# Gate passes of a graph GRU on 64-row halves of TensorE, with the x load, the xs load and the h copy moved

## The reference

```
adj = relu(x.reshape(b, 1600) @ masker_param + masker_bias)      # (b, 2, 50, 50)
adj = adj / (adj.sum(-1) + 1e-6)
m = adj @ (h @ weight)                                            # h starts as x
gates = m @ w_ih.T + b_ih + h @ w_hh.T + b_hh
r, z, ng = split(gates, 3)
h = (1 - sigmoid(z)) * tanh(sigmoid(r) * ng) + sigmoid(z) * h
h = batch_norm(h); h = layer_norm(h)
out = softmax(h @ attn_w.T + attn_b) @ h                          # (b, 2 * 32)
```

## Time and profile before

| | us |
|---|---|
| median of 3 runs (2510.01 to 2519.66) | 2515.34 |
| the profiled execution | 2501.48 |
| its span in the profile | 2499.7 |
| TensorE busy in the span | 2353.0 (94%) |
| VectorE, ScalarE, GpSimd busy | 1052.6, 817.7, 560.5 |
| granted TensorE clock, mean | 0.971 |

### The profile page before, as it was taken

The page is one execution under the profiler, slowest core; times in us unless marked ns, Lnnn a source line. Parts: engine busy times, 40 slices in busy tenths (PEclk is TensorE's granted clock), DMA queues, the critical chain, the costliest instruction groups (busy, mean ns, idle before and its releaser), DMA issues. The chain is left out here.

```text
span 2499.7 us, 34838 instructions
## 1 busy us (share of the span) xinstructions
PE 2353.0 (94%) x12466; PEld 1906.7 (76%) x12466; DVE 1052.6 (42%) x1787; ACT 817.7 (33%) x1369; POOL 560.5 (22%) x365
## 2 busy tenths in 40 slices
PE   8999999999999999999999966999999999965788
PEld 7888888888888888888888855888888888852333
DVE  5333222333352223333123313656666566674456
ACT  4222221222242222222122213445454444436340
POOL 0000000000000000000000000677676777764230
PEclk9999999999999999999999987999999999977899
DMA  6322122222242222211222024545555454327430
GB/s 219 118 86 85 31 81 86 86 86 86 80 147 88 86 86 84 84 55 59 86 86 83 28 72 133 159 137 162 154 148 161 134 168 139 117 82 224 125 91 5
DMA packets 137728, 264.14 MB, mean 106 GB/s; under 512 B 11590, under 2 KB 97382, under 8 KB 134374
## 3 DMA queue, kind: packets, MB, share of 16 engines
q1 hardware_dynamic: 121546, 237.24, 30.5%
q10 hardware_dynamic: 16128, 26.22, 3.0%
HBM read 195.72 MB, written 67.70 MB: 105 GB/s over the span
## 5 line engine op out<-in xcount | busy, mean ns | idle before, releaser
L344 PE MATMUL psum<-w_hi,x_lo 128*128 128x500 f32 x2080 | 820.9, 395 | 8.1 <-DVE w_lo L214 8.1
L344 PE MATMUL psum<-w_lo,x_hi 128*128 128x500 f32 (+1 forms) x2080 | 810.3, 390 | 0.0
L344 PE MATMUL psum<-w_hi,x_hi 128*128 128x500 f32 x1920 | 745.9, 388 | 0.0
L278 DVE TENSOR_REDUCE rows<-u 128x10 f32<-128x500 f32 x160 | 107.6, 672 | 917.5 <-ACT u L227 917.2
L344 PEld LDWEIGHTS psum<-w_hi,x_lo 128*128 128x128 f32 x2080 | 391.4, 188 | 83.8 <-issue 8.4
L344 PEld LDWEIGHTS psum<-w_lo,x_hi 128*128 128x128 f32 (+1 forms) x2080 | 392.0, 188 | 75.1
L344 PEld LDWEIGHTS psum<-w_hi,x_hi 128*128 128x128 f32 x1920 | 360.8, 188 | 73.2
L233 ACT COPY at<-psum 128x640 f32<-128x640 f32 x160 | 110.9, 693 | 699.5 <-PE psum L324 699.5
L638 POOL MEMSET share<- 128x1 f32 x1 | 0.1, 98 | 1484.2 <-POOLq L82 1484.2
L704 PE MATMUL psum<-adj_sb,xs_sb 100*64 100x100 f32 x2048 | 200.6, 350 | 32.5 <-DMA xs_sb<-xz 32.5
L227 ACT ACTIVATE u<-psum 128x500 f32<-128x500 f32 x160 | 94.0, 587 | 332.7 <-PE psum L344 332.7
(11 more groups left out here) (170 smaller groups left out, 2878.2 us busy)
## 6 DMA issues: line engine op xcount, KB each, us to landing
w_raw<-W SPq DMA_DIRECT2D x140, 500.0 KB, 6.8
adjT<-at SPq DMA_DIRECT2D x320, 125.0 KB
adj_sb<-adjT SPq DMA_DIRECT2D x16, 2500.0 KB
xs_sb<-xz SPq DMA_DIRECT2D x16, 1600.0 KB
hF<-hC ACTq DMA_DIRECT2D x96, 256.0 KB, 2.8
h<-hF SPq DMA_DIRECT2D x64, 256.0 KB, 4.1
xg_sb<-xg SPq DMA_DIRECT2D x16, 800.0 KB, 18.8
h<-hF SPq DMA_DIRECT2D x48, 192.0 KB, 3.7
```

The source lines that it names most:

```text
L278: nc.vector.tensor_reduce(rows[:, 0], u[:, c2], AX.X, ALU.add).then_inc(dve_step, 1)
L344: last = nc.tensor.matmul(mm_out(w % 2), a[0:r, k, cols], b[0:r, k, :], start=k == 0 and n == 0, stop=k == KF and n == 1)
```

## The change

1. **R and Z in row halves.** The weights of R and Z are packed in one array `wd[:, :, RZ_W]`: rows 0 to 63 (two blocks) hold R in columns 0 to 63 and Z in columns 64 to 127, rows 64 to 127 hold Z in columns 0 to 63 and R in columns 64 to 127. Each of the six products is issued twice, on rows 0 to 63 and on rows 64 to 127, with outputs in two banks, so 12 products of 64 rows take the place of 12 of 128. N stays as it was, now last, with the transposes ahead of it. Semaphores `rz_done` and `gates_done` take the place of one per gate, and the R/Z products wait for both sigmoids of the step before.
2. **ScalarE** does each sigmoid in two instructions of 64 partitions, from the two banks. The result of Z goes to one bank, so it first waits for the h of the step before (`h_ready`).
3. **The h copy** (`evacuate`) moves from ScalarE to VectorE, between `update` and `finish`; `store` moves behind tanh.
4. **The load of `xg`** is issued by ScalarE's queue, behind tanh of round 0 of the next tile, and no more by SyncE.
5. **`xs`** has the layout [100, 2, 2, 32, 64] and is loaded as two transfers of 50 partitions by 8 KB each for a tile, half of the bytes. The zeros are set once at the start by VectorE, and SyncE waits for them. A weight load now reads its 64 columns at a distance of 64 elements.

```diff
-        xs = sb("xs_sb", [2 * N, 2, SH, 2 * D])
+        xs = sb("xs_sb", [2 * N, 2, 2, D, SH])
...
-                sp.dma_start(xs[:, r], ins["xz"][tile]).then_inc(adj_loaded[r], 16)
+                for half in range(2):
+                    sp.dma_start(xs[N * half:N * half + N, r, half], ins["xm"][tile, half]).then_inc(adj_loaded[r], 16)
...
-                    sp.wait_ge(h_ready, (tile + 1) * ROUNDS)
-                    if more:
-                        load_xg(tile + 2, r)
...
             load_xg(0, 0)
+            sp.wait_ge(zeroed, 1)
             load_adj(0, 0)
...
+            def load_xg(tile, r):
+
+                act.wait_ge(h_ready, (tile - 1) * ROUNDS)
+                nc.scalar.dma_start(xg[:, r], ins["xg"][tile]).then_inc(xg_loaded[r], 16)
...
-                    act.wait_ge(gate_done[R_G], it * S + s + 1)
+                    act.wait_ge(rz_done, it * S + s + 1)
                     wait(act, n_in_ready, it * S + s)
-                    nc.scalar.activation(r_gate[:], gate_bank(R_G, s), ACT.Sigmoid,
-                                         bias=bias[:, R_G:R_G + 1]).then_inc(r_ready, 1)
-                    act.wait_ge(gate_done[Z_G], it * S + s + 1)
-                    nc.scalar.activation(gate_bank(Z_G, s), gate_bank(Z_G, s), ACT.Sigmoid,
-                                         bias=bias[:, Z_G:Z_G + 1]).then_inc(z_ready, 1)
+                    for pair in range(2):
+                        half = slice(SH * pair, SH * pair + SH)
+                        last = nc.scalar.activation(r_gate[half], rz_bank(pair)[half], ACT.Sigmoid, bias=bias[half, R_G:R_G + 1])
+                    last.then_inc(r_ready, 1)
+                    wait(act, h_ready, it * S + s)
+                    for pair in range(2):
+                        half, other = slice(SH * pair, SH * pair + SH), slice(SH - SH * pair, 2 * SH - SH * pair)
+                        last = nc.scalar.activation(z_bank[half], rz_bank(pair)[other], ACT.Sigmoid, bias=bias[other, Z_G:Z_G + 1])
+                    last.then_inc(z_ready, 1)
...
+            nc.vector.memset(xs[:].rearrange("p r h d b -> p (r h d b)"), 0.0).then_inc(zeroed, 1)
             nc.vector.memset(wd[:], 0.0).then_inc(zeroed, 1)
...
                     update(it, s)
+                    if s % ROUNDS and (s > ROUNDS or not (isinstance(it, int) and it == 0)):
+                        evacuate(it * 2 + s // ROUNDS - 1, s % ROUNDS - 1)
...
-                        last = nc.tensor.matmul(out_[SH * i:SH * i + SH, :, gi], xs[:, r, b, :], adj[:, r, :, b], start=True, stop=True)
+                        last = nc.tensor.matmul(out_[SH * i:SH * i + SH, :, gi], xs[:, r, :, :, b].rearrange("p h d -> p (h d)"), adj[:, r, :, b], start=True, stop=True)
...
+                wait(pe, r_ready, it * S + s)
+                wait(pe, z_ready, it * S + s)
+                for w, m, first, final in terms(RZ_W):
+                    for pair in range(2):
+                        half = slice(SH * pair, SH * pair + SH)
+                        last = nc.tensor.matmul(rz_bank(pair), w[half], m[half], start=first, stop=final)
+                last.then_inc(rz_done, 1)
+                if q and (r or not (isinstance(it, int) and it == 0)):
+                    turn_chunks(it * 2 + r - 1, q - 1)
+                wait(pe, h_ready, it * S + s - 1)
+                for w, m, first, final in terms(N_W):
+                    last = nc.tensor.matmul(n_bank(s), w, m, start=first, stop=final)
+                last.then_inc(gates_done, 1)
...
+            for n in range(len(batches)):
+                evacuate(TILES - 1, n)
```

More of the change, by code:

```diff
@@ L64 @@
 R_G, Z_G, N_G = 0, 1, 2
+RZ_W, N_W = 0, 1
 FQ = P // D
@@ L484, in x_hi @@
                     act.wait_ge(xg_loaded[r], (it + 1) * 16)
-                    wait(act, gate_done[Z_G], it * S if r else it * S - ROUNDS)
+                    wait(act, gates_done, it * S if r else it * S - ROUNDS)
                 g = slice(k * XG, (k + 1) * XG)
@@ L510, in turn @@
                     r, q = divmod(s, ROUNDS)
-                    if q and (r or not (isinstance(it, int) and it == 0)):
-                        evacuate(it * 2 + r - 1, q - 1)
                     if s + 1 < S or more:
-                        wait(act, gate_done[Z_G], it * S + s)
+                        wait(act, gates_done, it * S + s)
                         m_halves(it + (s + 1) // S, (s + 1) % S)
-                    if q and (r or not (isinstance(it, int) and it == 0)):
-                        store(it * 2 + r - 1, q - 1)
                     k = s % ROUNDS - (ROUNDS - 1 - XPARTS)
@@ L549, in _ @@
                 q = slice(D * j, D * j + D)
-                nc.vector.tensor_copy(wd[q, 0, :, q], psum[q, 0:3 * D].rearrange("p (g e) -> p g e", g=3))
-                last = nc.vector.tensor_copy(wd[q, 1, :, q], whh4[q, :].rearrange("p (g e) -> p g e", g=3))
+                pair, one = divmod(j, 2)
+                at = {R_G: SH * pair + D * one, Z_G: SH - SH * pair + D * one, N_G: D * j}
+                for gate, first in at.items():
+                    of, e = (N_W if gate == N_G else RZ_W), slice(D * gate, D * gate + D)
+                    nc.vector.tensor_copy(wd[q, 0, of, first:first + D], psum[q, e])
+                    last = nc.vector.tensor_copy(wd[q, 1, of, first:first + D], whh4[q, e])
             last.then_inc(blocks_ready, 1)
@@ L587, in finish, with evacuate @@
                                         n_gate.rearrange("p (c g) -> p c g", g=QB), ALU.add).then_inc(h_ready, 1)
+            def evacuate(tile, n):
+                dve.wait_ge(turned, tile * len(batches) + n + 1)
+                wait(dve, hC_stored[n], 16 * tile)
+                c0, c1 = batches[n]
+                nc.vector.tensor_copy(hC[:, c0:c1, :].rearrange("p c b -> p (c b)"),
+                                      turn_bank[:, 0:(c1 - c0) * P]).then_inc(hC_ready, 1)
             def turn_rows(it, r, k):
@@ L712, in gates @@
                 if s == ROUNDS - 2:
-                    pe.wait_ge(adj_loaded[1], (it + 1) * 32)
+                    pe.wait_ge(adj_loaded[1], (it + 1) * 48)
                 if s == S - 2 and more:
-                    pe.wait_ge(adj_loaded[0], (it + 2) * 32)
+                    pe.wait_ge(adj_loaded[0], (it + 2) * 48)
                 pe.wait_ge(m_ready, it * S + s + 1)
                 xb = [t[:, r, q].unsqueeze(1).to_broadcast([P, T, N * QB]) for t in (xg_hi, xg_lo)]
-                for gate in (R_G, N_G, Z_G):
-                    if gate == Z_G:
-                        if q and (r or not (isinstance(it, int) and it == 0)):
-                            turn_chunks(it * 2 + r - 1, q - 1)
-                        wait(pe, h_ready, it * S + s - 1)
-                    elif gate == N_G:
-                        wait(pe, h_ready, it * S + s - 1)
-                    else:
-                        wait(pe, r_ready, it * S + s)
-                    terms = []
-                    for part, (hi, lo) in enumerate(((m_hi[:, s % 2], m_lo[:, s % 2]), xb)):
-                        terms += [(wd_lo[:, part, gate], hi), (wd_hi[:, part, gate], lo), (wd_hi[:, part, gate], hi)]
-                    for i, (w, m) in enumerate(terms):
-                        last = nc.tensor.matmul(gate_bank(gate, s), w, m, start=i == 0, stop=i == len(terms) - 1)
-                    last.then_inc(gate_done[gate], 1)
@@ L1353 @@
         "fold": np.tile(np.eye(D, dtype=x.dtype), (4, 4)),
-        "xz": pairs(x),
+        "xm": x.reshape(TILES, 2, 2, 32, N, D).transpose(0, 2, 4, 5, 1, 3).reshape(TILES, 2, N, D, SH),
         "xg": x.reshape(TILES, 4, ROUNDS, QB, N, D).transpose(0, 1, 5, 2, 4, 3).reshape(TILES, P, ROUNDS, N * QB),
```

47 lines of the change are left out of this document (22 added, 25 removed).

## The result

The changed kernel takes 2471.37 us (median of 4 runs, 2470.29 to 2473.66) against 2514.14 (4 runs, 2510.01 to 2519.66) before: ratio 0.9831, 95% interval 0.9808 to 0.9854. The profiled execution takes 2470.29 us, its span is 2468.5, 31.2 less than the span before. The medians differ by 42.8: the profiled execution of before stood 12.7 under its median, outside the range of the four runs, and this one 1.1 under. So what the two traces show side by side is 31 of the 43 us.

What follows compares the result with a forecast made beforehand. TensorE bounds stage 2, GpSimd's loop nearly as long and the next bound. Tiles 1 to 14 -31, tile 0 -5, last tile -4, start -3, end +7: -36 from 2515.3, forecast 2479 us; own range 2450 to 2503, wider 2445 to 2522.

Steps and rivals of the forecast that it cites:

- What bounds: Stage 2: TensorE bounds before at 42.4 us a tile; GpSimd's loop, 43.2 before, becomes the new tile.
- it binds even now: Stage 2 before the change: GpSimd's loop of 43.2 us a tile already binds, 0.8 above TensorE's 42.4.
- Pairs: R and Z products: the two row halves run side by side, 0.20 us a pair (0.18 to 0.21), 1.2 a step.
- further changes of form: TensorE's step: one more change from pairs to whole arrays costs 0.10 us.
- The stride: Aggregate weights read every 64 elements: 0.15 us a step, between nothing and 0.5.
- The loop: From tile to tile through GpSimd: 8.9 + 7.3 + GpSimd's unchanged 24.1 = 40.3 us, before the clock charge.
- The clock: TensorE after its 3.6 us idle before each tile: slow clock charged 1.5 us a tile, lower end 0.
- a few us late are covered by the 3.6 of idleness: x load: a small delay is hidden by TensorE's 3.6 us idle before each tile, so its cost is nothing.
- bytes ahead are fewer by 0.8 MB: x load: fewer bytes are queued ahead of x; the x load as a whole was costed at nothing.
- x comes late: Slower rival: x takes 20.6 us like a 64 KB store, 7 a tile behind the cover, 2577 us; chance 0.03.
- ScalarE and VectorE: Stage 2: split sigmoids and the moved copy are covered; uncovered, at most 0.5 and 0.1 us a step.
- The end: End of stage 2: seven copies delay VectorE's last statistics about 11.5 us, operations running alone give 4.5 back; +7.

Runs made afterwards that it cites:

- x_lo_early: Changed kernel with GpSimd's four x_lo put between the second and third of its last four folding steps: 2445.28 us, ratio 0.9741.
- before_x_lo_early: Kernel before the change with x_lo moved in among GpSimd's last folding steps: 2514.07 us, ratio 1.0004.
- xs_as_before: Changed kernel with xs as before, one contiguous 1600 KB transfer a tile with its zeros: 2514.0 us, ratio 1.0009.
- fill_the_wait: Changed kernel with 16 superfluous products in front of the wait for xg_lo, from the third tile on: 2455.27 us, ratio 0.977.
- copies_on_scalar: Changed kernel with the h copies back on ScalarE, the last tile's seven too: 2472.48 us, ratio 0.9844.
- x_first_xs_as_before: Changed kernel with x_lo early, x ahead of adj on SyncE's queue, last tile's copies on ScalarE and xs as before: 2497.08 us, ratio 0.9908.
- halves_in_turn: Changed kernel with all six products of rows 0 to 63 ahead of the six of rows 64 to 127: 2493.04 us, ratio 0.9936.

## Why the prediction was right, point by point

Forecast 2479 us, measured 2471.4. The forecast took 36 us off the median of before. From trace to trace it is 31.2, 5 short of that, and from median to median 42.8, 7 beyond it, since the profiled execution of before was an unusually short one. That the two errors have different signs and 2471 still lies near 2479 is in part luck; the terms are judged by the traces.

| term | forecast | in the trace |
|---|---|---|
| first aggregate (1521.00 to 1518.22) | -3 | -2.8 |
| from there to the first gate of tile 1 | -5 | -4.9 |
| tiles 1 to 14 (614.8 to 584.7) | -31 | -30.1 |
| tile 15, first gate to last block transposes (43.8 to 40.05) | -4 | -3.7 |
| end of stage 2 | +7 | +6.4 |
| stage 3 | 0 | +3.9 |

*What bounds.* GpSimd's loop does become the bound: x_lo_early takes 26 us out, and the wait stands in the trace with 3 us. But for the kernel before "it binds even now" was too strong: there the early `x_lo` moved nothing that shows (before_x_lo_early).

*Pairs.* 0.18, the lower end; I took 0.20. The row of column groups was read as two groups; there are four, for at 2350.55 four products start within 0.02 us and the next four 0.45 later, so it spoke for the lower end too. The Trainium skill, page "TensorE: Matmul & The Clock Gate", Part 3, gives some 4 ns for each further product; by it a pair is an estimated 0.184. The trace agrees: the two halves start 0.003 apart and the pairs 0.184 in the median. With all pairs and N at 0.18, xs_as_before leaves 4.48 - (5.39 - 2.16 + 1.08) = 0.17 for the further changes of form, where I had 0.10.

*The stride.* Mis-sized: 0.30 a step (4.78 against 4.48 in xs_as_before), twice the 0.15 that I took. The load grows from 153 to 221 ns, so the columns' part grows 2.4 times, about as my upper end assumed; but of these 0.07 only 0.04 a pair show in the step, so the upper end of 0.5 was not reached. The Trainium skill, "SBUF — State Buffer", Door 1, says that each fp32 on a new 16-byte line pays; the trace agrees, with 68 ns for 64 columns.

These three make the step 4.78 in place of 4.68, and TensorE's tile 37.5 in place of 36.7. It cost little, as GpSimd set the tile.

*The loop.* Forecast 40.3 + 1.5 = 41.8, measured 42.0. The first part is 17.7 (forecast 8.9 + 7.3 + 1.5), GpSimd's 24.3 (24.1).

*The clock.* Forecast 1.5 a tile. In fill_the_wait, with the clock at 1.00, the first step is 0.9 to 1.9 shorter, though it holds 3.1 us of products where the wait was 2.7 to 3.0; the loop's first part is 17.7 in place of the 16.2 without this charge. The mechanism is shown, the size is right.

*The x load.* Here a step failed: "a few us late are covered by the 3.6 of idleness" is true from tile 5 on, where x is issued 16.8 us behind `adj`, lands 26.9 behind it and is asked for at 27.7 (the load at 1726.16). It is not in tiles 1 to 3: without the idle stretch x is issued 12.9 behind `adj`, lands 13.5 to 14.4 later, and round 3 waits. It did not show in the sum, because GpSimd's loop does not bind those tiles yet: from first gate product to first gate product, as the forecast counts, tiles 1 to 4 took 163.5 us where it had 165.7, and tiles 5 to 14 took 421.2 where it had 418. And I had priced the smaller `xs` as "bytes ahead are fewer by 0.8 MB", at nothing: xs_as_before shows that it carries some 43 us of the result. The rival "x comes late" had its mechanism right but the wrong number: in the changed kernel the 64 KB store lands after 16.9 us and the x load, on the same queue, after 10.1, so the store is no measure of it. Why the store takes so long is not shown.

*ScalarE and VectorE.* Covered, as forecast; the copy on VectorE shows in the loop (1735.38 to 1736.05, just ahead of L588). Had the copies stayed on ScalarE, tiles would be about 0.6 longer (copies_on_scalar, 42.7 in the mean of tiles 5 to 14 against 42.1).

*The end.* As forecast: seven copies hold VectorE up. The last reduction starts at 2197.23; the block transposes began at 2182.31. Before, those began at 2223.78 and the reduction at 2227.39, so it now comes 11.3 us later. Timeline of the changed kernel, VectorE:

```profile
2182.31 3.69 DVE L611 STREAM_TRANSPOSE hT<-hG 128x800 f32<-128x800 f32 x4
...
2187.85 0.69 DVE L601 COPY hC<-psum 128x512 f32<-128x512 f32 x1 [1.27 <-PE psum L765]
...
2197.23 2.14 DVE L643 TENSOR_REDUCE means<-hG 128x60 f32<-128x1920 f32 x1
...
2199.64 2.16 DVE L648 TENSOR_TENSOR hG<-hG,means 128x1920 f32<-128x1920 f32 x1
```

The subtraction takes 2.16 where it took 4.33 beside GpSimd. It and the two operations around it give back 4.9 us, the gain that I had set against it.

*Stage 3.* 3.9 us more, not forecast. 2.3 of them are VectorE's longer wait for the small constants (`t_mask`, 4.45 against 2.13 us); the rest was not traced further.

What stays open: why 4900 KB take about 31 us although the DMA share is 0.5 in the mean and 0.6 to 0.75 in the middle of these loads in x_first_xs_as_before (no run loads one of the three alone), and how far the loads could be shortened by another shape.

## What to carry to other kernels

Two parts of a change can each be worth nothing and together be worth the whole: ask of every limit next to the one that is lifted what it would be by itself, in us a tile, the loads' too. Where a wait in front of TensorE repeats, its price is its length and the slow clock behind it. A transfer that never shows as a wait may still be late once its issue moves, here by 13 us: compare issue to landing with issue to use, not with zero.

## What the runs showed of the hardware

- Products on the two row halves, each chain to its own bank, run side by side at 0.18 us a pair of 400 columns, though both write all 128 output partitions; and they do so in part even when the program has one chain behind the other (halves_in_turn). The Trainium skill, page "TensorE: Matmul & The Clock Gate", Part 3, states that matmuls start strictly in program order; the trace disagrees: the second half's first product starts at 1800.14, the first half's fourth at 1800.31.
- A weight load of 64 columns, each 256 bytes from the next, takes 221 ns against 153 (medians), which costs 0.30 us a step of 16 such loads.
- Eleven idle stretches of 2.7 to 3.0 us in front of a tile were each followed by a granted clock of 0.50 for 3.4 or 6.8 us, and so were three of 1.2 to 2.0 us in round 3 of the changed kernel; in the kernel before one of 1.9 us was not. Superfluous products in the gap made the kernel 16 us faster.
